# Moving steps within VectorE's and ScalarE's order at the batch ends of a Strassen pair loop

## The chip, the cores and the metric

One core of one Trainium2 chip. The metric is the device time of one execution in microseconds (us), lower is better. Engines are named as in the profile: PE (TensorE), DVE (VectorE), ACT (ScalarE), POOL (GpSimd), SP (SyncE, which issues the DMAs here).

## The reference

The input `x` is (8, 512, 64, 64) in float32. It is one attention block with pooled keys and values, all in float32:

```python
qk  = relu(bn(einsum('bchw,oc->bohw', x, qk_w)))      # 256 channels
val = relu(bn(einsum('bchw,oc->bohw', x, v_w)))       # 512 channels
key   = psp(qk)                       # adaptive max pools 1, 3, 6, 8: 110 cells
value = psp(val).transpose(0, 2, 1)
query = qk.reshape(B, 256, 4096).transpose(0, 2, 1)
scores = softmax(einsum('bnc,bcs->bns', query, key) * 256 ** -0.5)
y = einsum('bns,bsc->bnc', scores, value)             # to (B, 512, H, W)
return x + bn(einsum('bchw,oc->bohw', y, out_w))
```

## The kernel before

**Tiles.** Each of the 8 batches has 8 tiles of 512 positions, 64 tiles in all. Every float32 product is split into a high part (rounded to fp32r) and a low part (the rest), so one product of 128x128 weights with a 128x512 tile is three matmuls, hi*hi, lo*hi, hi*lo. ACT makes the high parts, POOL and DVE the low parts.

**Strassen pairs.** Tiles are taken two at a time, a pair step `s` from 1 to 27 (`PAIRS` is 28), and the convolutions of a pair are made with Strassen's scheme (Winograd's form) in three products `j` = 0, 1, 2 (two halves of the values' channels, then the queries' and keys'). `pair_product(s, j, fill1, ..., fill4)` is PE's order for one: P1 (3 matmuls), `fill1`, P5 (3), U2 (3), U1 (9), `fill2`, U3 (3), U5 (9), `fill3`, U6 (9), U7 (6), `fill4`. The fills are attention work of older tiles: `project` (probabilities times values times output weights, 3 matmuls), `sums` (row sums of the exponentials, 2), `scores` (6). Between them other engines make sums of PSUM banks: `copy_u1` and `copy_u5` (ACT, L851 and L857), `make_u4` (DVE, L1217), which U3 waits for, and `make_u7` (DVE, L1223), which U6 waits for before its first matmul.

**Attention** runs behind the convolutions: in step `s`, `A = 2s-8` and `B0 = A-1` are the tiles whose attention is done. For a tile `a`: `exps`, `split_e_lo` (L1286), `sums` (PE), `guess` (ACT, L925 and L927: a logarithm and an exponential give a reciprocal), `refine` (DVE, L1272 and L1275: one Newton step), `normalise` (L1281), `split_p_hi` (ACT, L931), `split_p_lo` (DVE, L1291), four `project`s, each followed by `add_out` (DVE, L1298), which adds the residual and frees the bank: `project(a, 2)` waits for `add_out(a, 0)`.

**Batch ends.** Where A is a multiple of 8 (s = 4, 8, 12, 16, 20, 24) a batch's tiles are complete (`batch_ended`). Then `finish_grids(VC, CC)` and `finish_keys` (L1237 to L1251) end the pooling of the keys, which `scores(A)` needs; `finish_grids(0, VC)` and `finish_values` end that of the values; PE multiplies values and output weights (`turn_values`, 12 matmuls, fill3 of j = 1), `make_values` (DVE), `values_hi` (ACT, L936) and `values_lo` (DVE, L1306) follow, and `project(A, 0)` (fill3 of j = 2) needs their result and `split_p_lo(A)`. Rows of each product are pooled by `pool_pair_rows` (DVE, L1157), groups of rows by `pool_cells` (L1195 to L1202). At s = 4 there is no `B0`.

**Loads of the pair.** `split_part_hi(s, i)` (ACT, L844) and `split_part_lo` (POOL, L449) split the nine parts of the next pair's data; POOL also makes four sums of tiles (L459 to L462, L468) and the queries' low part (L479). SP loads the next pair's tiles when part 6 and part 7 of this pair have their low part, and after that stores results and loads residuals in a ring of three buffers.

**Order.** Each engine's queue is in order, written out by hand as a list of calls per step; semaphores connect the engines. All of a step that an engine reaches waits behind what stands ahead of it in that list. Nothing plans the order at run time.

Of the kernel before, what the change touches and what calls it, by code (L numbers as in the profile page):

```python
# [26 lines left out]
def psp_attention(nc, x, qk_w, v_w, out_w, bn_in_rows, out):  # L27
# [14 lines left out]
    NT = 8  # L42
    TN = H * W // NT
    KC = CIN // P
    VC, QC, OC = CV // P, CK // P, CIN // P
# [13 lines left out]
    with ExitStack() as ctx:  # L59
# [748 lines left out]
        def _(act):  # L808
# [20 lines left out]
            def split_part_hi(s, i):  # L829

                raw, b0, b1 = PARTS[i]
                if i in (1, 2, 4, 8):
                    act.wait_ge(t_made, 4 * (s - 1) + {1: 1, 2: 2, 4: 3, 8: 4}[i])
                else:
                    wait_x(act, 2 * s + (1 if i in (5, 7) else 0))
                if s == 1:
                    if i not in (1, 2, 8):
                        act.wait_ge(conv_done, CC if i in (0, 3, 6) else 2 * CC)
                else:
                    n, g = product(s - 1, 2), pair_group(s - 1, 2)  # L840
                    used, count = [(p1_done, n), (p5_done, n), (u2_done, n), (conv_done, g), (u3_done, n),
                                   (conv_done, g + 1), (x0_used, n), (conv_done, g + 3), (conv_done, g + 2)][i]
                    act.wait_ge(used, count + 1)
                nc.scalar.activation(xh[:, b0:b1, :], raw, ACT.Copy).then_inc(x_hi, 1)  # L844

            def copy_u1(s, j):
                n = product(s, j)
                u1, _, u6, _ = pair_banks(n)
                act.wait_ge(p1_done, n + 1)
                act.wait_ge(rows_pooled, pair_group(s, j) - 2)  # L850
                nc.scalar.activation(u6[:, :], u1[:, :], ACT.Copy).then_inc(u1_copied, 1)  # L851

            def copy_u5(s, j):
                n = product(s, j)
                act.wait_ge(p5_done, n + 1)
                wait(act, u7_made, n)
                nc.scalar.activation(u5[:, :], pair_banks(n)[3][:, :], ACT.Copy).then_inc(u5_copied, 1)  # L857
# [63 lines left out]
            def guess(a):  # L921

                act.wait_ge(sums_done, a + 1)
                wait(act, p_made, a)
                nc.scalar.activation(r0[:, :], sum_ps[:, :], ACT.Ln).then_inc(ln_done, 1)  # L925
                act.wait_ge(ln_done, a + 1)
                nc.scalar.activation(r0[:, :], r0[:, :], ACT.Exp, scale=-1.0).then_inc(guess_made, 1)  # L927

            def split_p_hi(a):
                act.wait_ge(p_made, a + 1)  # L930
                nc.scalar.activation(e_slot(a)[0], score_bank(a)[:, :], ACT.Copy).then_inc(p_hi, 1)  # L931

            def values_hi(k):
                act.wait_ge(vo_made, k + 1)
                wait(act, out_done, OC * NT * k)
                nc.scalar.activation(vo_h[:, :], vo[:, :], ACT.Copy).then_inc(vo_hi, 1)  # L936
# [26 lines left out]
            for s in range(1, PAIRS):  # L963
                A = 2 * s - NT
                B0 = A - 1
                nxt = s + 1 if s + 1 < PAIRS else None
                copy_u1(s, 0)
                copy_u5(s, 0)
                if s > 1:
                    split_part_hi(s, 7)  # L970
                split_part_hi(s, 8)
                if B0 >= 0:
                    guess(B0)
                if A >= 0:
                    split_q_hi(A)
                if B0 >= 0:
                    split_p_hi(B0)
                copy_u1(s, 1)
                copy_u5(s, 1)
                if A >= 0:  # L980
                    exps(A)
                    split_q_hi(A + 1)
                if A >= 0 and A % NT != 0:
                    guess(A)
                    split_p_hi(A)
                copy_u1(s, 2)
                copy_u5(s, 2)
                if A >= 0 and A % NT == 0:
                    guess(A)
                    values_hi(A // NT)  # L990
                    split_p_hi(A)
                if nxt:
                    for i in range(4):
                        split_part_hi(nxt, i)
                store_pair_q(s, 0)
                if nxt:
                    split_part_hi(nxt, 4)
                    split_part_hi(nxt, 5)
                else:
                    split_hi(LAST, 0)  # L1000
                store_pair_q(s, 1)
                if A >= 0:
                    exps(A + 1)
                if nxt:
                    split_part_hi(nxt, 6)
                else:
                    split_hi(LAST, 1)
                store_pair_q(s, 2)
                store_pair_q(s, 3)
# [53 lines left out]
        def _(dve):  # L1063
# [277 lines left out]
            for s in range(1, PAIRS):  # L1341
                A = 2 * s - NT
                B0 = A - 1
                t0 = 2 * s % NT
                batch_ended = A >= 0 and A % NT == 0
                if s == 1:
                    pool_tile_cells(1, 0, CC)
                else:
                    pool_cells((t0 - 2) % NT, VC, CC, pair_group(s, 0))
                    pool_cells((t0 - 1) % NT, VC, CC, pair_group(s, 0))  # L1350
                make_u4(s, 0)
                if B0 >= 0:
                    refine(B0)
                    normalise(B0)
                pool_pair_rows(s, 0, 0)
                make_u7(s, 0)
                if A >= 2:
                    add_out(A - 2, 2)
                    add_out(A - 2, 3)
                if B0 >= 0:  # L1360
                    split_p_lo(B0)
                pool_pair_rows(s, 0, 1)
                if batch_ended:
                    finish_grids(VC, CC)
                    finish_keys()
                pool_pair_rows(s, 0, 2)
                pool_pair_rows(s, 0, 3)
                if B0 >= 0:
                    add_out(B0, 0)
                    add_out(B0, 1)  # L1370
                make_u4(s, 1)
                if batch_ended:
                    if B0 >= 0:
                        add_out(B0, 2)
                    finish_grids(0, VC)
                    finish_values(0, VC)
                    pool_pair_rows(s, 1, 0)
                    make_u7(s, 1)
                    split_e_lo(A)
                    pool_pair_rows(s, 1, 1)  # L1380
                    make_values(A // NT)
                    pool_pair_rows(s, 1, 2)
                    pool_pair_rows(s, 1, 3)
                else:
                    if A >= 0:
                        split_e_lo(A)
                    pool_pair_rows(s, 1, 0)
                    make_u7(s, 1)
                    if B0 >= 0:
                        add_out(B0, 2)  # L1390
                    pool_pair_rows(s, 1, 1)
                    if A >= 0:
                        refine(A)
                    pool_pair_rows(s, 1, 2)
                    if A >= 0:
                        normalise(A)
                    pool_pair_rows(s, 1, 3)
                    pool_cells(t0, 0, VC, pair_group(s, 2))
                    pool_cells(t0 + 1, 0, VC, pair_group(s, 2))
                    if A >= 0:  # L1400
                        split_p_lo(A)
                make_u4(s, 2)
                if B0 >= 0:
                    add_out(B0, 3)
                if batch_ended:
                    refine(A)
                    normalise(A)
                    pool_cells(t0, 0, VC, pair_group(s, 2))
                    pool_cells(t0 + 1, 0, VC, pair_group(s, 2))
                    values_lo(A // NT)  # L1410
                pool_pair_rows(s, 2, 0)
                make_u7(s, 2)
                if batch_ended:
                    split_p_lo(A)
                elif A >= 0:
                    add_out(A, 0)
                    add_out(A, 1)
                pool_pair_rows(s, 2, 1)
                if batch_ended:
                    add_out(A, 0)  # L1420
                if A >= 0:
                    split_e_lo(A + 1)
                pool_pair_rows(s, 2, 2)
                pool_pair_rows(s, 2, 3)
                if batch_ended:
                    add_out(A, 1)
# [119 lines left out]
```

## Time and profile before

| | us |
|---|---|
| median of 3 runs | 1461.75 (1459.16 to 1464.56) |
| the profiled execution | 1460.46 |
| its span, first to last instruction | 1458.7 |
| PE busy | 1371.6 (94%) |
| DVE busy | 973.6 (67%) |
| POOL busy | 753.5 (52%) |
| ACT busy | 632.2 (43%) |
| mean granted PE clock | 0.981 |
| DMA queues, share of 16 engines | 44% |

Matmuls are pipelined, each starts before the last has ended, so a busy PE is one that is being fed, and its rate is read from counts over a stretch.

### The profile page before, as it was taken

Reading aid. Unit: us, or ns where it says so; the run is one execution under the profiler, and the core shown is the slowest. Engines: PE = TensorE matmul, PEld = TensorE weight load, DVE = VectorE, ACT = ScalarE, POOL = GpSimd, SP = SyncE. Lnnn points to the kernel's source line nnn. Section 1 sums busy time; section 2 is a strip of 40 time slices with the busy share of each in tenths; the row PEclk is TensorE's granted clock in tenths of the full one; section 3 lists DMA queues with packets and bytes.
Section 4 is the critical chain, followed back from the end, with each engine's and each line's share of the span. In section 5 each row is a group of like instructions: output and inputs, shape, how many; then the busy total and the mean of one; then the engine's idle time right before and its main releaser. Section 6 shows DMA issues by size and latency. Waiting matters only on the chain. (4 is left out here: it accounts for less than half of the span.)

```text
span 1458.7 us, 17069 instructions
## 1 busy us (share of the span) xinstructions
PE 1371.6 (94%) x5786; PEld 1091.5 (75%) x5786; DVE 973.6 (67%) x2262; ACT 632.2 (43%) x991; POOL 753.5 (52%) x469
## 2 busy tenths in 40 slices
PE   7999889998899988999899997999979999999997
PEld 6777677786677867777677776777767777788885
DVE  6554567667667676676766766666766677877566
ACT  4233344542445524545245453345434454764422
POOL 2555566552655526555256552565524643675532
PEclk9999999999999999999999999999989999999999
DMA  5211144443444434544345442455424553898426
GB/s 188 87 58 58 58 145 144 142 144 101 162 156 141 137 109 151 166 141 133 110 144 173 151 144 81 144 173 165 143 69 144 173 173 116 275 317 274 145 87 231
DMA packets 110344, 213.46 MB, mean 146 GB/s; under 512 B 6538, under 2 KB 6578, under 8 KB 110258
## 3 DMA queue, kind: packets, MB, share of 16 engines
q1 hardware_dynamic: 109682, 211.33, 43.9%
q8 instruction: 46, 0.75, 0.2%
q10 hardware_dynamic: 576, 1.05, 0.2%
q14 instruction: 40, 0.33, 0.1%
HBM read 145.25 MB, written 67.11 MB: 146 GB/s over the span
## 5 line engine op out<-in xcount | busy, mean ns | idle before, releaser
L449 POOL TENSOR_TENSOR xl<-xa,xh 128x512 fp32r<-128x512 f32 x162 | 267.6, 1669 | 336.7 <-ACT xh L844 336.7
L1157 DVE TENSOR_REDUCE row_max<-conv_ps 128x64 f32<-128x384 f32 (+2 forms) x576 | 287.4, 529 | 212.2 <-ACT q L904 95.1
L570 PE MATMUL conv_ps<-xh,wh 128*128 128x512 f32 x891 | 353.9, 397 | 13.0 <-DVE conv_ps L1223 12.7
L572 PE MATMUL conv_ps<-xl,wh 128*128 128x512 f32 x891 | 350.1, 393 | 0.0
L571 PE MATMUL conv_ps<-xh,wl 128*128 128x512 f32 x891 | 348.7, 391 | 0.0
L479 POOL TENSOR_TENSOR q_l<-q,q_h 128x1024 fp32r<-128x1024 f32 x64 | 154.1, 2407 | 193.6 <-ACT q_h L910 193.6
L570 PEld LDWEIGHTS conv_ps<-xh,wh 128*128 128x128 f32 x891 | 168.9, 190 | 61.0 <-DVE conv_ps L1223 23.9
L572 PEld LDWEIGHTS conv_ps<-xl,wh 128*128 128x128 f32 x891 | 168.1, 189 | 37.5
L571 PEld LDWEIGHTS conv_ps<-xh,wl 128*128 128x128 f32 x891 | 168.7, 189 | 36.1
L851 ACT ACTIVATE conv_ps<-conv_ps 128x512 f32<-128x512 f32 x81 | 47.4, 585 | 260.2 <-PE conv_ps L572 260.2
L1298 DVE TENSOR_TENSOR xo<-out_ps,xo 128x512 f32<-128x512 f32 x226 | 148.2, 682 | 7.2 <-PE out_ps L663 6.4
L844 ACT ACTIVATE xh<-xa 128x512 fp32r<-128x512 f32 x162 | 123.9, 771 | 65.9 <-PE conv_ps L572 65.9
L570 PE MATMUL conv_ps<-xh,sh 128*128 128x512 f32 x324 | 133.3, 411 | 8.1 <-DVE row_max L1157 7.0
L661 PE MATMUL out_ps<-e_h,vo_h 128*128 128x512 f32 x218 | 91.3, 419 | 46.3 <-DVE e_l L1291 24.9
L572 PE MATMUL conv_ps<-xl,sh 128*128 128x512 f32 x324 | 129.2, 399 | 0.0
L571 PE MATMUL conv_ps<-xh,sl 128*128 128x512 f32 x324 | 128.9, 398 | 0.0
L1217 DVE TENSOR_TENSOR conv_ps<-conv_ps,u 128x512 f32<-128x512 f32 x81 | 56.4, 697 | 98.8 <-PE conv_ps L572 54.6
L443 POOL TENSOR_TENSOR xl<-xa,xh 128x1024 fp32r<-128x1024 f32 x34 | 81.5, 2409 | 62.1 <-ACT xh L827 62.1
L449 POOL TENSOR_TENSOR xl<-tt,xh 128x512 fp32r<-128x512 f32 x81 | 107.8, 1331 | 0.0
L857 ACT ACTIVATE u<-conv_ps 128x512 f32<-128x512 f32 x81 | 48.6, 599 | 113.0 <-PE conv_ps L572 112.9
L557 PE MATMUL conv_ps<-xh,wh 128*128 128x512 f32 x240 | 95.2, 397 | 0.0
L559 PE MATMUL conv_ps<-xl,wh 128*128 128x512 f32 x240 | 94.4, 393 | 0.0
(218 smaller groups left out, 2312.8 us busy)
## 6 DMA issues: line engine op xcount, KB each, us to landing
xa<-x SPq DMA_DIRECT2D x148, 512.0 KB, 4.6
xo<-x SPq DMA_DIRECT2D x115, 512.0 KB, 4.6
out<-xo SPq DMA_DIRECT2D x115, 512.0 KB, 3.1
q<-x SPq DMA_DIRECT2D x8, 512.0 KB, 4.6
out<-q SPq DMA_DIRECT2D x8, 512.0 KB, 3.2
q<-v_w ACTq DMA_DIRECT2D x4, 256.0 KB, 4.7
q<-out_w SPq DMA_DIRECT2D x1, 1024.0 KB, 6.9
out<-xa SPq DMA_DIRECT2D x2, 512.0 KB, 3.3
```

The costliest lines, as they stand in the source:

```text
L443: nc.gpsimd.tensor_tensor(xl[:, b:b + 2, :], xa[:, part, s % 2, :, :], xh[:, b:b + 2, :], ALU.subtract)\
L449: nc.gpsimd.tensor_tensor(xl[:, b0:b1, :], raw, xh[:, b0:b1, :], ALU.subtract).then_inc(x_lo, 1)
L479: nc.gpsimd.tensor_tensor(q_l[:, :, :], q[:, a % NT, :, :], q_h[:, :, :], ALU.subtract).then_inc(q_lo, 1)
L557: nc.tensor.matmul(bank(s, c)[:, :], wh[:, k, cols], hi, start=(k == 0), stop=False)
L559: last = nc.tensor.matmul(bank(s, c)[:, :], wh[:, k, cols], lo, start=False, stop=(k == KC - 1))
L570: nc.tensor.matmul(out[:, :], hi, xh[:, b, :], start=start, stop=False, skip_group_check=True)
L571: nc.tensor.matmul(out[:, :], lo, xh[:, b, :], start=False, stop=False, skip_group_check=True)
L572: return nc.tensor.matmul(out[:, :], hi, xl[:, b, :], start=False, stop=stop, skip_group_check=True)
L661: nc.tensor.matmul(bk[:, :], vo_h[:, cols], hi, start=True, stop=False)
L844: nc.scalar.activation(xh[:, b0:b1, :], raw, ACT.Copy).then_inc(x_hi, 1)
L1157: last = nc.vector.tensor_reduce(row_max[:, c, n, :], src[:, r0_ * W:r1_ * W].rearrange("p (r w) -> p w r", w=W), AX.X, ALU.max)
L1298: nc.vector.tensor_tensor(xt, out_bank(a, m)[:, :], xt, ALU.add).then_inc(out_added, 1)
```

## The change

Only the order of calls on two engines is changed, ACT (`block.scalar`) and DVE (`block.vector`); no instruction is added, removed or altered, and PE's, POOL's and SP's lists are the same.

On ACT: `copy_u5(s, 0)` goes behind part 7's split, `guess(B0)` ahead of part 8's; at batch ends `guess(A)` goes ahead of `copy_u1(s, 2)`, and parts 0 and 1 of the next pair go between `values_hi` and `split_p_hi(A)`. On DVE: at batch ends `finish_grids(VC, CC)` goes ahead of `refine(B0)`, `finish_keys` behind `add_out(B0, 0)` and `add_out(B0, 1)`, `refine(A)` ahead of `make_u4(s, 2)`, `values_lo` and `split_p_lo(A)` ahead of the cells' pooling. In every step `make_u7(s, 0)` goes directly behind `refine(B0)`.

```diff
--- before.py
+++ after.py
@@ -965,12 +965,12 @@
                 B0 = A - 1
                 nxt = s + 1 if s + 1 < PAIRS else None
                 copy_u1(s, 0)
-                copy_u5(s, 0)
                 if s > 1:
                     split_part_hi(s, 7)
-                split_part_hi(s, 8)
+                copy_u5(s, 0)
                 if B0 >= 0:
                     guess(B0)
+                split_part_hi(s, 8)
                 if A >= 0:
                     split_q_hi(A)
                 if B0 >= 0:
@@ -983,15 +983,21 @@
                 if A >= 0 and A % NT != 0:
                     guess(A)
                     split_p_hi(A)
+                batch_ended = A >= 0 and A % NT == 0
+                if batch_ended:
+                    guess(A)
                 copy_u1(s, 2)
                 copy_u5(s, 2)
-                if A >= 0 and A % NT == 0:
-                    guess(A)
+                if batch_ended:
                     values_hi(A // NT)
+                if nxt:
+                    split_part_hi(nxt, 0)
+                    split_part_hi(nxt, 1)
+                if batch_ended:
                     split_p_hi(A)
                 if nxt:
-                    for i in range(4):
-                        split_part_hi(nxt, i)
+                    split_part_hi(nxt, 2)
+                    split_part_hi(nxt, 3)
                 store_pair_q(s, 0)
                 if nxt:
                     split_part_hi(nxt, 4)
@@ -1349,25 +1355,27 @@
                     pool_cells((t0 - 2) % NT, VC, CC, pair_group(s, 0))
                     pool_cells((t0 - 1) % NT, VC, CC, pair_group(s, 0))
                 make_u4(s, 0)
+                if batch_ended:
+                    finish_grids(VC, CC)
                 if B0 >= 0:
                     refine(B0)
+                make_u7(s, 0)
+                if B0 >= 0:
                     normalise(B0)
                 pool_pair_rows(s, 0, 0)
-                make_u7(s, 0)
                 if A >= 2:
                     add_out(A - 2, 2)
                     add_out(A - 2, 3)
                 if B0 >= 0:
                     split_p_lo(B0)
                 pool_pair_rows(s, 0, 1)
-                if batch_ended:
-                    finish_grids(VC, CC)
-                    finish_keys()
                 pool_pair_rows(s, 0, 2)
                 pool_pair_rows(s, 0, 3)
                 if B0 >= 0:
                     add_out(B0, 0)
                     add_out(B0, 1)
+                if batch_ended:
+                    finish_keys()
                 make_u4(s, 1)
                 if batch_ended:
                     if B0 >= 0:
@@ -1399,25 +1407,29 @@
                     pool_cells(t0 + 1, 0, VC, pair_group(s, 2))
                     if A >= 0:
                         split_p_lo(A)
+                if batch_ended:
+                    refine(A)
                 make_u4(s, 2)
+                if batch_ended:
+                    normalise(A)
                 if B0 >= 0:
                     add_out(B0, 3)
                 if batch_ended:
-                    refine(A)
-                    normalise(A)
+                    values_lo(A // NT)
+                    split_p_lo(A)
+                    make_u7(s, 2)
+                    pool_pair_rows(s, 2, 0)
+                    pool_pair_rows(s, 2, 1)
                     pool_cells(t0, 0, VC, pair_group(s, 2))
                     pool_cells(t0 + 1, 0, VC, pair_group(s, 2))
-                    values_lo(A // NT)
-                pool_pair_rows(s, 2, 0)
-                make_u7(s, 2)
-                if batch_ended:
-                    split_p_lo(A)
-                elif A >= 0:
                     add_out(A, 0)
-                    add_out(A, 1)
-                pool_pair_rows(s, 2, 1)
-                if batch_ended:
-                    add_out(A, 0)
+                else:
+                    pool_pair_rows(s, 2, 0)
+                    make_u7(s, 2)
+                    if A >= 0:
+                        add_out(A, 0)
+                        add_out(A, 1)
+                    pool_pair_rows(s, 2, 1)
                 if A >= 0:
                     split_e_lo(A + 1)
                 pool_pair_rows(s, 2, 2)
```

## Rows read from the trace of the kernel before

**Rows 1.** The page, busy time of each engine.
```profile
PE 1371.6 (94%) x5786; PEld 1091.5 (75%) x5786; DVE 973.6 (67%) x2262; ACT 632.2 (43%) x991; POOL 753.5 (52%) x469
```

**Rows 2.** Waits of PE: us in total, times, longest us.
```profile
PE out_ps L661 <- DVE e_l L1291: 24.9, 7, 3.9
PE out_ps L661 <- DVE xo L1298: 21.4, 7, 4.2
PE conv_ps L570 <- DVE conv_ps L1223: 12.7, 23, 0.6
...
PE conv_ps L570 <- DVE row_max L1157: 7.0, 7, 2.6
```

**Rows 3.** Windows: stretch, its us, each engine's busy us (count), PEclk, DMA share, GB/s.
```profile
207.60:1192.40 984.80, 932.54 (x3910) 741.92 (x3910) 663.46 (x1520) 431.69 (x687) 518.84 (x331) 0.98 0.44 142
375.70:517.90 142.20, 140.01 (x601) 111.67 (x600) 97.83 (x225) 66.32 (x104) 81.57 (x52) 1.00 0.50 163
389.30:429.10 39.80, 39.80 (x173) 31.87 (x171) 26.64 (x62) 19.55 (x31) 21.94 (x16) 1.00 0.46 148
...
331.70:388.40 56.70, 47.96 (x187) 37.91 (x187) 37.20 (x89) 19.82 (x32) 23.97 (x16) 0.91 0.33 110
```

**Rows 4.** Timeline of PE at two batch ends (s = 24, s = 4): start, us, what.
```profile
1063.01 0.79 PE L661 MATMUL out_ps<-e_h,vo_h 128*128 128x512 f32 x1 [4.08 <-DVE xo L1298]
1063.60 0.63 PE L662 MATMUL out_ps<-e_h,vo_l 128*128 128x512 f32 x1
1064.03 0.63 PE L663 MATMUL out_ps<-e_l,vo_h 128*128 128x512 f32 x1
...
1080.46 0.39 PE L645 MATMUL sum_ps<-e_l,ones 128*128 128x512 f32 x1
...
1092.33 0.62 PE L661 MATMUL out_ps<-e_h,vo_h 128*128 128x512 f32 x1 [3.95 <-DVE e_l L1291]
...
190.23 0.50 PE L661 MATMUL out_ps<-e_h,vo_h 128*128 128x512 f32 x1 [3.54 <-DVE e_l L1291]
```

**Rows 5.** Timeline of ACT in step s = 24.
```profile
1044.62 0.58 ACT L851 ACTIVATE conv_ps<-conv_ps 128x512 f32<-128x512 f32 x1
1046.48 0.60 ACT L857 ACTIVATE u<-conv_ps 128x512 f32<-128x512 f32 x1 [1.28 <-PE conv_ps L572]
1046.98 1.05 ACT L844 ACTIVATE xh<-xa 128x1024 fp32r<-128x1024 f32 x1
...
1049.07 0.63 ACT L927 ACTIVATE r<-r 128x512 f32<-128x512 f32 x1
...
1082.97 0.60 ACT L857 ACTIVATE u<-conv_ps 128x512 f32<-128x512 f32 x1 [0.81 <-PE conv_ps L572]
```

**Rows 6.** Timeline of DVE in step s = 24.
```profile
1047.23 0.70 DVE L1217 TENSOR_TENSOR conv_ps<-conv_ps,u 128x512 f32<-128x512 f32 x1 [0.28 <-ACT u L857]
1049.73 0.70 DVE L1272 SCALAR_TENSOR_TENSOR sum_ps<-sum_ps,r 128x512 f32<-128x512 f32 x1 [1.80 <-ACT r L927]
...
1052.40 0.69 DVE L1223 TENSOR_TENSOR conv_ps<-conv_ps,u 128x512 f32<-128x512 f32 x1
...
1055.77 0.20 DVE L1238 TENSOR_TENSOR rows<-cells 128x36 f32<-128x36 f32 x1
1056.00 1.16 DVE L1239 TENSOR_TENSOR cells<-rows 128x18 f32<-128x18 f32 x1
1057.19 0.17 DVE L1240 TENSOR_REDUCE cells<-cells 128x2 f32<-128x18 f32 x1
...
1060.64 0.39 DVE L1251 TENSOR_TENSOR key_l<-key_d,key_h 128x220 fp32r<-128x220 f32 x1
...
1088.36 1.01 DVE L1202 TENSOR_REDUCE part<-row_max 128x8 f32<-128x88 f32 x6
```

**Rows 7.** Timeline of POOL in step s = 24.
```profile
1048.10 2.41 POOL L449 TENSOR_TENSOR xl<-xa,xh 128x1024 fp32r<-128x1024 f32 x1 [2.62 <-ACT xh L844]
...
1055.81 1.32 POOL L459 TENSOR_TENSOR tt<-xa 128x512 f32<-128x512 f32 x1 [1.69 <-DMA xa<-x]
```

## The prediction

> **What bounds the kernel.** First the page's busy times [rows 1]: PE is busy for 1371.6 of 1458.7 us, and the next engine, DVE, for 973.6. So the time is PE's work plus what PE waits, 87 us in all. Second, the waits of PE [rows 2]: two groups of seven, each with a longest wait near 4 us (behind `split_p_lo`, L1291, and behind `add_out`, L1298), 23 short ones of 0.6 us at most (U6 waiting for `make_u7`, L1223), and one of 2.6 us among those behind row pooling. Third, the windows [rows 3]. A stretch without a wait runs 173 matmuls in 39.80 us, 0.230 us each; a stretch with three of the short waits and one batch of ordinary steps takes 142.20 us with 140.01 busy for 601, 0.233 each. A step with a batch end takes 56.70 us for 187 matmuls, though 187 x 0.233 is only 43.6, and its granted clock is 0.91. Of the 13.1 us too many, 4.08 and 3.95 are the two long waits [rows 4] and 0.5 to 0.6 is the short one. The rest, some 4.5 us, is the clock: behind the wait the matmuls start 0.43 us apart (1063.60 to 1064.03), twice the usual distance, so TensorE has gone from 2.4 to 1.2 GHz after pausing some 4 us.
>
> **The first wait and its removal** (s = 24; the steps s = 8, 12, 16, 20 look alike). `project(B0, 2)` is ready 4.08 us before 1063.01, at 1058.93. Before it, DVE works off `finish_grids` and `finish_keys`, from before 1055.77 to 1061.03 [rows 6], then three row poolings and `add_out(B0, 0)`. After the change the grids fill a hole: behind `make_u4`, which starts at 1047.23, DVE now idles 1.80 us for `guess` [rows 6]. ACT's new order also makes `guess` sooner: it follows `copy_u5` at 1046.48 directly, so it ends at about 1046.48 + 0.5 + 1.2 = 1048.2 instead of 1049.7 [rows 5].
>
> What the grids cost there needs a look at POOL. L1239 took 1.16 us at 1056.00 and ended at 1057.16, 0.03 after POOL's L459 (1055.81 + 1.32 = 1057.13), while L1238 started before it and took 0.20 [rows 6, 7]. The reduction L1240 is not held. So such an instruction waits for the POOL instruction in flight. POOL's split of part 7 is issued 0.5 us behind `copy_u1` at 1044.62, and 1.05 us later POOL has it: 1046.2 to 1048.6 (2.41 us [rows 7]). L1237, at about 1047.83, then ends at 1048.7, L1238 runs to 1048.9, L1239 meets POOL's split of part 8 (from 1048.84, 1.3 us) and ends at 1050.2, L1240 at 1050.4. `refine` takes two steps of 0.73 us, `make_u7` 0.69: U7 is there at 1052.6. PE wants it at 1053.14 less 0.5, at 1052.65. The short wait shrinks to nothing, or to 0.1 to 0.2 us.
>
> Behind that, one instruction each 0.6 us: `normalise` 1052.5, a row, two `add_out`, `split_p_lo` until 1055.5, five row reductions until 1057.5, `add_out(B0, 0)` done at 1058.2. PE, 0.5 us earlier than before, wants it at 1058.4. The first long wait goes. `finish_keys` follows the second `add_out` at 1058.8. The next tiles' loads are issued when part 7 has its low part, now 1.9 us sooner, so POOL's L459 to L462 run from about 1054 to 1058 and no longer meet the keys, which take 3.6 us now (1057.36 to 1061.03 [rows 6]), two of them held as L1239 is; I estimate 1.7 us for six that aren't held, at 0.2 to 0.4 each as L1238 and L1251. They end at 1060.5, U2 at the same time, so `make_u4(s, 1)` isn't late, and `scores(A)` wants keys at 1062.4. Slack there is 1.9 us. `values` follow as before, with the `add_out(B0, 2)` ahead of them; its residual is loaded behind a store that DVE releases at 1054.9, and lands about 5 us later, against a use at 1061.2.
>
> **The second wait.** `project(A, 0)` waits for `split_p_lo(A)`. Its chain is `sums(A)`, `guess(A)` (1.2 us), `refine`, `normalise`, `split_p_hi`, `split_p_lo`. Today `guess(A)` stands behind `copy_u5(s, 2)` at 1082.97 [rows 5], which ends 2.7 us after `sums(A)` has; and between `split_p_hi` and `split_p_lo` DVE pools cells (the last six of them 1.01 us [rows 6], 2.3 in all), makes `values_lo`, waits for a row and makes U7. With the change `guess` starts when `sums(A)` is done, at about X = 1080.46 + 0.39 = 1080.85 [rows 4]. `copy_u1(s, 2)` is pushed back behind it, done at X + 1.8, where U2 wants it at X + 1.9. `refine` is done at X + 2.8 and `make_u4` starts at X + 2.9, as now. Then `normalise`, `add_out`, `values_lo` (perhaps held 0.5 us by POOL's split of part 0), `split_p_lo` done at X + 6.3, U7 at X + 6.9. PE ends U5 and wants the first at X + 7.5, the second 2 us later. The cells' 2.3 us lie behind the two row poolings then, with `split_e_lo(A+1)` behind them at about X + 13, and `sums(A+1)` wants it at X + 15. The second wait goes, and with it the slow clock.
>
> **Other steps.** 17 ordinary steps lie between 207.60 and 1192.40. There `guess` is 1.5 us sooner and `make_u7` right behind `refine`, so U7 is made when U3 is done, about 1.3 us before PE wants it. The 0.5 to 0.6 us wait goes in each.
>
> **The sum.** From 207.60 to 1192.40 PE runs 3910 matmuls [rows 3]. At 0.233 us each, a rate that still has short pauses in it, that is 911 us instead of 984.8: 74 us less. (At 0.230, without any, 900 and 85 less: the lower bound of the time.) The short wait of s = 5 just before gives 0.6. At s = 4 there is no `B0` and no fill of it: I count its second wait, 3.54 us [rows 4] and 1.4 of slow clock; its 2.6 us wait I count at nothing, since there POOL is late with four splits, the grids end near 159.5 and U6 waits about 2 us instead. Sum 74 + 0.6 + 5 = 79.6 us. The steps from s = 28 on and the start stay. 1460.5 - 79.6 = 1380.9. The profiled execution stands 1.3 us below the median of the runs, which is noise here: I say 1381.
>
> **A rule beside it.** POOL and DVE meet in the rows above. The Trainium skill, "SBUF — State Buffer", Who interferes with whom, says that a DVE instruction with two SBUF inputs, or in a two-port mode, and a GpSimd instruction lock each other out for the whole instruction, whoever comes first, and that reductions don't take part. It speaks against this change, which sets the grids into a stretch where POOL is at work; the trace agrees with it (L1239 held, L1240 not). Without such a lock the grids would end near 1048.7 and PE's waits would be as summed above.
>
> **Rivals.** *The grids are held twice.* L1238 starts about 0.1 us before POOL's split of part 8 in my working. If POOL is first, L1238 ends at 1050.2, and L1239 comes behind the start of POOL's 2.4 us for the queries and ends at 1052.6. Then U7 is at 1054.8, U6 waits 2.1 us, and all behind shifts with it. For: 0.1 us is thin. Against: the distances from `copy_u1` to `copy_u5` and `make_u4` that it hangs on come from engine chains and not from DMAs. Price 5 x 2.1 = 10.5 us: 1392. *One long wait comes back.* `copy_u1` behind `guess(A)` has 0.1 us of slack, `add_out(B0, 2)` and its residual under 1 us. If one of the two long waits stays in the five steps, with its clock, 5 x (4 + 2.2) = 31 us come back: 1412. *The waits only move.* If the chain behind them (keys, then values) was as late as they are, nothing is gained: 1461. Against it stands the slack of 1.9 us and more at each. *Slower: the clock.* With the pauses gone PE runs some 1000 us on end. If the chip took it to the lower level for part of that, each matmul would cost 0.43 - 0.23 = 0.2 us more; from 400 matmuls (of 3910) on the gain is eaten, at 450 the kernel is 10 us slower, 1471. Against: it held 1.00 through 601 matmuls from 375.70 to 517.90 [rows 3].
>
> **How the numbers follow.** Forecast 62%, grids held twice 22%, one wait back 11%, waits only move 3%, slower by the clock 2%. About 0.5% (7 us) is what a measurement can tell here. Both first cases and the third lie far below that line, so faster 0.95, same 0.03, slower 0.02. The range goes from 1371, a little above the bound with no pause at all (85 + 5.6 less is 1370), to 1402, past the 1392 of the first rival and halfway to the third case.
>
> **What would show it.** Right: PE's waits for L1298 and L1291 at batch ends gone from its list, those for L1223 under 3 us in total, PEclk 1.00 in batch steps of about 43.6 us, ordinary steps of 40.7, L1239 held once to about 1.2 us. Wrong: L1239 or L1238 at 2.4 us and U6 waiting 2 us behind L1223; or waits of PE at L570 (U2) for ACT L851, or new ones of 3 us and more anywhere with a clock of 0.9 behind them.

## The result and the profile after

| | before | after |
|---|---|---|
| median of 4 runs, us | 1462.55 | 1374.34 (1374.09 to 1377.43) |
| profiled execution, us | 1460.46 | 1374.09 |
| its span, us | 1458.7 | 1372.3 |
| mean granted PE clock | 0.981 | 0.999 |

The ratio is 0.9404, with a 95% interval from 0.9381 to 0.9427: 88.2 us less by the medians, 86.4 by the spans of the two profiled executions. 1381 was forecast, 1371 to 1402 was the range.

The page after, busy time of each engine (the answer to [rows 1]):

```profile
PE 1341.9 (98%) x5786; PEld 1077.6 (79%) x5786; DVE 967.1 (70%) x2262; ACT 633.3 (46%) x991; POOL 755.5 (55%) x469
```

The matmuls are the same. PE is busy for 30 us less (it ran some of them at the lower clock before) and idle for 57 us less. The waits of PE after, to be held against [rows 2] (L1163 is the old L1157, L1229 the old L1223, L1297 the old L1291, L1304 the old L1298):

```profile
PE conv_ps L570 <- DVE row_max L1163: 4.6, 7, 1.0
...
PE conv_ps L570 <- DVE conv_ps L1229: 2.2, 1, 2.2
...
PE out_ps L661 <- DVE e_l L1297: 1.7, 1, 1.7
...
PE out_ps L661 <- DVE xo L1304: 0.9, 2, 0.7
```

46.3 us of waiting for L1298 and L1291 have become 2.6, and the 23 short waits for U7 have become a single one. What is left for L1297 (1.7) stands in the first step behind the pairs, which the change does not touch. The windows after, for [rows 3] (stretch, its us, each engine's busy us and count, PEclk, DMA share, GB/s):

```profile
205.00:1109.90 904.90, 904.90 (x3909) 728.41 (x3908) 653.68 (x1518) 432.57 (x687) 520.88 (x330) 1.00 0.47 154
982.70:1026.20 43.50, 43.50 (x190) 35.09 (x189) 34.50 (x86) 20.06 (x33) 24.32 (x16) 1.00 0.39 129
1026.20:1066.70 40.50, 40.50 (x177) 32.63 (x176) 28.11 (x65) 19.59 (x32) 23.59 (x16) 1.00 0.53 177
```

In the first, all of 904.90 us is busy: through 3909 matmuls, five batch ends among them, the profile lists no wait of PE, and the clock is the upper one throughout. The second lies over a batch end, the third over an ordinary step. An ordinary step has 175 matmuls (the window counts two that its ends cut), so 40.50 us are 0.231 each; counted by their starts the batch end has the same 0.231.

How DVE goes through the batch end s = 24 after the change, and POOL beside it (start, us, what; for [rows 6, 7]):

```profile
978.11 0.70 DVE L1223 TENSOR_TENSOR conv_ps<-conv_ps,u 128x512 f32<-128x512 f32 x1 [0.28 <-ACT u L857]
978.71 0.91 DVE L1243 TENSOR_TENSOR cells<-part 128x72 f32<-128x72 f32 x1
979.66 0.20 DVE L1244 TENSOR_TENSOR rows<-cells 128x36 f32<-128x36 f32 x1
979.89 1.16 DVE L1245 TENSOR_TENSOR cells<-rows 128x18 f32<-128x18 f32 x1
981.08 0.17 DVE L1246 TENSOR_REDUCE cells<-cells 128x2 f32<-128x18 f32 x1
...
982.63 0.69 DVE L1229 TENSOR_TENSOR conv_ps<-conv_ps,u 128x512 f32<-128x512 f32 x1
```

```profile
977.12 2.42 POOL L449 TENSOR_TENSOR xl<-xa,xh 128x1024 fp32r<-128x1024 f32 x1 [0.75 <-ACT xh L844]
979.71 1.30 POOL L449 TENSOR_TENSOR xl<-tt,xh 128x512 fp32r<-128x512 f32 x1 [0.17 <-ACT xh L844]
```

L1243 meets POOL's split of part 7 and ends when that ends (979.54, 979.62). L1244 starts 0.05 us ahead of the split of part 8 and is free. L1245 meets that split and ends with it (1.16 us). The order of these three is the one worked out before, and its thin place is the 0.05 us. U7 is made at 983.32, and PE takes it up at once:

```profile
983.38 0.50 PE L570 MATMUL conv_ps<-xh,wh 128*128 128x512 f32 x1
983.72 0.40 PE L571 MATMUL conv_ps<-xh,wl 128*128 128x512 f32 x1
```

No wait is listed, but the second matmul stands 0.34 us behind the first and not 0.23, as it does behind a short wait. Since a matmul counts as busy for 0.39 us and the next one starts after 0.23, a pause of up to 0.16 us does not show as idle. So U7 comes just in time here, with nothing to spare.

### The profile page after: what moved, and what is told of

Same layout as the page of the kernel before. It is cut to its first block, busy times and chain, and to the rows that moved or that the text cites. A ratio compares the mean times of both kernels' runs of the same rounds, so it can differ in the third digit from the quotient of the medians.

```text
span 1372.3 us, 17075 instructions
## 1 busy us (share of the span) xinstructions
PE 1341.9 (98%) x5786; PEld 1077.6 (79%) x5786; DVE 967.1 (70%) x2262; ACT 633.3 (46%) x991; POOL 755.5 (55%) x469
## 4 chain that ended last, share of the span: by engine, by line
PE 88%; DVE 3%; ACT 1%; issue 1%; DVEq 0%; ACTq 0%
PE conv_ps L570 20%; PE conv_ps L572 19%; PE conv_ps L571 19%; PE out_ps L661 4%; PE out_ps L662 4%; PE out_ps L663 4%; PE conv_ps L559 3%; PE conv_ps L557 3%; PE conv_ps L558 3%; PE score_ps L634 2%; PE score_ps L633 2%; PE score_ps L632 2%; PE sum_ps L644 1%; PE sum_ps L645 1%; PE sum_ps L672 0%
## 5 line engine op out<-in xcount | busy, mean ns | idle before, releaser
L1163 DVE TENSOR_REDUCE row_max<-conv_ps 128x64 f32<-128x384 f32 (+2 forms) x576 | 285.5, 528 | 196.1 <-ACT q L904 91.2
L571 PE MATMUL conv_ps<-xh,wl 128*128 128x512 f32 x891 | 347.8, 390 | 0.0
L479 POOL TENSOR_TENSOR q_l<-q,q_h 128x1024 fp32r<-128x1024 f32 x64 | 154.1, 2408 | 175.6 <-ACT q_h L910 175.6
L1304 DVE TENSOR_TENSOR xo<-out_ps,xo 128x512 f32<-128x512 f32 x226 | 148.1, 681 | 1.6 <-PE out_ps L663 0.7
L925 ACT ACTIVATE r<-sum_ps 128x512 f32<-128x512 f32 x64 | 38.2, 596 | 146.8 <-PE sum_ps L645 146.8
L1223 DVE TENSOR_TENSOR conv_ps<-conv_ps,u 128x512 f32<-128x512 f32 x81 | 56.4, 696 | 66.8 <-PE conv_ps L572 55.9
L558 PE MATMUL conv_ps<-xh,wl 128*128 128x512 f32 x240 | 93.9, 391 | 0.0
```

The lines of the kernel that those rows point to most:

```text
L479: nc.gpsimd.tensor_tensor(q_l[:, :, :], q[:, a % NT, :, :], q_h[:, :, :], ALU.subtract).then_inc(q_lo, 1)
L558: nc.tensor.matmul(bank(s, c)[:, :], wl[:, k, cols], hi, start=False, stop=False)
L571: nc.tensor.matmul(out[:, :], lo, xh[:, b, :], start=False, stop=False, skip_group_check=True)
L1163: last = nc.vector.tensor_reduce(row_max[:, c, n, :], src[:, r0_ * W:r1_ * W].rearrange("p (r w) -> p w r", w=W), AX.X, ALU.max)
L1304: nc.vector.tensor_tensor(xt, out_bank(a, m)[:, :], xt, ALU.add).then_inc(out_added, 1)
```

## The experiments

Nine kernels start from the changed one, one from the kernel before, and two build on one of these. All medians are of four or five runs, and each ratio is to the kernel before, run beside it. Differences to the changed kernel (1374.34 us) are between medians taken at different times; the median of the kernel before moved by 1.3 us over them (1461.89 to 1463.21), so 1 to 2 us are not to be told apart.

### Undoing the order of keys and grids (first long wait)

```diff
                 make_u4(s, 0)
-                if batch_ended:
-                    finish_grids(VC, CC)
...
                 pool_pair_rows(s, 0, 1)
+                if batch_ended:
+                    finish_grids(VC, CC)
+                    finish_keys()
                 pool_pair_rows(s, 0, 2)
...
-                if batch_ended:
-                    finish_keys()
                 make_u4(s, 1)
```

> The changed kernel with finish_grids(VC, CC) and finish_keys back between the row poolings of product 0. Theory: the wait of project(B0, 2) for add_out comes back at 5 batch ends, 3.5 to 4 us each, 18 to 20 us, and with it the slow clock, up to 2.2 us each: 1393 to 1405. Rival, the first wait was removed by the sooner guess and make_u7 and not by the keys' place: under 3 us more.

Measured 1400.33 us (ratio 0.9575, 0.9561 to 0.9589): 26.0 more than the changed kernel. The wait is back in the list, 20.2 us, at most 4.3:

```profile
PE out_ps L661 <- DVE xo L1304: 20.2, 7, 4.3
```

### Undoing the order in product 2 (second long wait)

On ACT `guess(A)` goes back behind `copy_u5(s, 2)` and parts 0 and 1 behind `split_p_hi(A)`; on DVE the old block of product 2 stands again:

```diff
-                if batch_ended:
-                    refine(A)
                 make_u4(s, 2)
...
+                    refine(A)
+                    normalise(A)
+                    pool_cells(t0, 0, VC, pair_group(s, 2))
+                    pool_cells(t0 + 1, 0, VC, pair_group(s, 2))
+                    values_lo(A // NT)
+                pool_pair_rows(s, 2, 0)
+                make_u7(s, 2)
+                if batch_ended:
+                    split_p_lo(A)
```

> The changed kernel with the order of product 2 at batch ends as before, on both engines (guess(A) behind copy_u5, parts 0 to 3 behind split_p_hi(A), the cells ahead of values_lo). Theory: project(A, 0) waits again for split_p_lo(A), 4 us at 6 batch ends and 1.4 to 2.5 us of slow clock each: 1406 to 1413.

Measured 1409.18 us (0.9635, 0.962 to 0.9649), 34.8 more.

```profile
PE out_ps L661 <- DVE e_l L1291: 25.3, 7, 4.3
```

25.3 - 1.7 = 23.6 us of waiting are back at six batch ends, and 34.8 us of time. Most of the difference is the clock, see the doses below.

### What carries the short waits: three undoings and one edit alone

`make_u7(s, 0)` back behind `normalise` and the first row:

```diff
                     refine(B0)
-                make_u7(s, 0)
-                if B0 >= 0:
                     normalise(B0)
                 pool_pair_rows(s, 0, 0)
+                make_u7(s, 0)
```

> The changed kernel with make_u7(s, 0) back behind normalise and the first row. Theory: in ordinary steps the sooner guess alone keeps U7 on time (made 1.0 us before PE wants it), at 5 batch ends U7 is 1.2 us late behind grids and refine: 6 to 7 us more, 1381. Rival, make_u7's place carried the ordinary steps: 14 us more and above.

Measured 1381.12 us (0.9448, 0.9432 to 0.9464), 6.8 more; five waits of 1.16 to 1.18 us at batch ends and 2.79 at s = 4, none in an ordinary step.

ACT's first reorder undone:

```diff
-                if s > 1:
-                    split_part_hi(s, 7)
                 copy_u5(s, 0)
-                if B0 >= 0:
-                    guess(B0)
+                if s > 1:
+                    split_part_hi(s, 7)
                 split_part_hi(s, 8)
+                if B0 >= 0:
+                    guess(B0)
```

> The changed kernel with ScalarE's first reorder undone: copy_u5(s, 0) first, then parts 7 and 8, then guess(B0). Theory: in ordinary steps U7 is still made at about 1.9 us behind refine's start, 0.7 us before PE wants it, so nothing is lost there. At batch ends the grids meet GpSimd's split of part 7 instead of part 8: if L1238's successor gets in ahead of it, refine is 0.3 us late and nothing is lost, if not 1.6 us at 5 batch ends. 1374 to 1382. Rival, the sooner guess carried the gain of the short waits: 14 us more, 1388.

Measured 1375.71 us (0.9407, 0.9393 to 0.9421), against 1374.34: no difference that stands out. Five waits of 0.28 us came, and the one at s = 4 went.

Both undone:

> The changed kernel with both of these undone: ScalarE's first reorder (guess again behind parts 7 and 8) and make_u7(s, 0) directly behind refine. Theory, each alone keeps U7 on time in ordinary steps, so undoing both brings back what neither alone did: 0.8 us in 18 ordinary steps, and 1.5 to 2 us at 5 batch ends, 22 to 25 us: 1396 to 1400. Rival, the short waits went with the long ones: as the run with only make_u7 back, 1381 to 1383.

Measured 1402.54 us (0.9594, 0.9574 to 0.9614), 28.2 more, against 22 to 25 expected. The waits for U7:

```profile
PE conv_ps L570 <- DVE conv_ps L1229: 21.7, 23, 5.1
```

The 18 ordinary ones are 0.5 to 0.6 us long as in the kernel before, four batch ends have 1.60, and the fifth has 5.11. There DVE's three maxima lost their race against POOL (DVE, then POOL):

```profile
827.82 2.41 DVE L1243 TENSOR_TENSOR cells<-part 128x72 f32<-128x72 f32 x1
830.26 1.19 DVE L1244 TENSOR_TENSOR rows<-cells 128x36 f32<-128x36 f32 x1
831.49 2.26 DVE L1245 TENSOR_TENSOR cells<-rows 128x18 f32<-128x18 f32 x1
```

```profile
827.73 2.41 POOL L449 TENSOR_TENSOR xl<-xa,xh 128x1024 fp32r<-128x1024 f32 x1 [2.63 <-ACT xh L844]
830.10 1.30 POOL L449 TENSOR_TENSOR xl<-tt,xh 128x512 fp32r<-128x512 f32 x1
831.35 2.36 POOL L479 TENSOR_TENSOR q_l<-q,q_h 128x1024 fp32r<-128x1024 f32 x1
```

POOL's first instruction starts 0.09 us ahead of L1243, and each of the three waits for one whole POOL instruction: 5.9 us for what takes 0.6 unhindered. This is the rival "the grids are held twice" and one more, in one step of five. In the other four L1243 starts 0.26 to 0.28 us ahead of POOL and takes 0.22, L1244 0.20, and only L1245 is held (2.28 us).

The edit alone, on the kernel before:

```diff
                     refine(B0)
-                    normalise(B0)
-                pool_pair_rows(s, 0, 0)
                 make_u7(s, 0)
+                if B0 >= 0:
+                    normalise(B0)
+                pool_pair_rows(s, 0, 0)
```

> The kernel before with one edit: make_u7(s, 0) directly behind refine(B0). Theory: U6's short waits of 0.5 to 0.6 us and the restart behind them go in the 18 ordinary steps (41.3 us to 40.5 each), the long waits stay: 13 to 14 us less, near 1449. Rival, the short wait is caused by guess being late and not by make_u7's place: no change, 1462.

Measured 1443.25 us (0.9863, 0.9848 to 0.9878): 19.7 less than the kernel before beside it, 17.5 by the spans, more than the 13 to 14 expected. The short waits are gone. The first long wait grew from 21.4 to 24.8 us in sum, presumably since PE reaches it sooner and DVE does not:

```profile
PE out_ps L661 <- DVE xo L1298: 24.8, 7, 4.8
```

All of PE's waits in sum fell by 10.5 us (81.8 to 71.3). The rest goes with the number of waits, 23 fewer: each short wait costs some 0.27 us more than its listed length, 0.16 hidden in the busy time of the matmul before it and 0.11 at the restart. That is an estimate from the distances 0.23, 0.34 and 0.39 above, and it gives 10.5 + 23 x 0.27 = 16.7 of the 17.5.

So either of the two edits alone keeps U7 on time in ordinary steps, and only without both does it come late. Their effects do not add.

### Where the grids stand, and what holds them

`finish_grids(VC, CC)` directly ahead of `finish_keys`, behind the second `add_out`:

```diff
                 make_u4(s, 0)
-                if batch_ended:
-                    finish_grids(VC, CC)
...
                 if batch_ended:
+                    finish_grids(VC, CC)
                     finish_keys()
                 make_u4(s, 1)
```

> The changed kernel with finish_grids(VC, CC) directly ahead of finish_keys, behind both add_outs, so away from GpSimd's splits. Theory: keys are 0.8 us later, still before scores(A) want them, and U6's wait of 2.2 us at s = 4 goes: 1372. Rival, the place in ScalarE's hole was needed: scores(A) wait about 1 us at 5 batch ends, 1379.

Measured 1371.31 us (0.9379, 0.9364 to 0.9394), 3.0 less; the intervals of the two ratios overlap, but all four runs lie below all four of the changed kernel. The place in DVE's idle time behind `make_u4` was not needed: the keys have the slack. At s = 4 the wait moved, though: U6's 2.2 us went and `scores` wait 2.0 us for the keys.

```profile
PE score_ps L632 <- DVE key_l L1257: 2.6, 2, 2.0
```

Compared matmul by matmul, the profiled execution is 1.9 us ahead of the changed kernel's behind s = 4 and gains 0.4 us more at each of the five other batch ends, though neither profile lists a wait for U7 there: 0.1 us of it is the restart at U6 (the 0.34 us above), another 0.1 one of the same kind at 989.04, where `project` comes just behind `add_out`, and the rest is in smaller pieces. At s = 4 nothing is gained in waiting (2.0 for 2.2 us); what went are the slow matmuls that follow U6's wait in the changed kernel, see the clock below. The grids still meet POOL in three steps: L1243, L1244 and L1245 take 1.30, 1.29 and 1.20 us at s = 4, ahead of the keys that are late there, and L1243 0.51 and 0.78 at s = 16 and 20, where no wait comes of it.

The same maxima as reductions:

```diff
-grid_chain(nc.vector.tensor_tensor(g6, part6[:, cs, 0::2, :], part6[:, cs, 1::2, :], ALU.max))
+grid_chain(nc.vector.tensor_reduce(g6, part6[:, cs, :, :].rearrange("p c (r t) w -> p c r w t", t=2), AX.X, ALU.max))
```

and in the same way for `rows3` and `g3`.

> The changed kernel with the grids' three maxima of two tensors written as reductions of one tensor over pairs, which have one SBUF input. Theory: they aren't held by GpSimd's instruction in flight, take about 0.2 to 0.3 us each also at L1245 and at s = 4, and U6's wait of 2.2 us at s = 4 goes: 1372. Rival, they are held as well (then the hold isn't one of the second input): 1374 or above.

Measured 1370.24 us (0.937, 0.9356 to 0.9384), 4.1 less, the best median here. At s = 8 (DVE, then POOL):

```profile
316.28 0.30 DVE L1243 TENSOR_REDUCE cells<-part 128x72 f32<-128x144 f32 x1
316.61 0.23 DVE L1244 TENSOR_REDUCE rows<-cells 128x36 f32<-128x72 f32 x1
316.87 0.19 DVE L1245 TENSOR_REDUCE cells<-rows 128x18 f32<-128x36 f32 x1
```

```profile
314.71 2.40 POOL L449 TENSOR_TENSOR xl<-xa,xh 128x1024 fp32r<-128x1024 f32 x1 [0.76 <-ACT xh L844]
```

POOL is at work from 314.71 to 317.11, over all three, and they take 0.30, 0.23 and 0.19 us. With two SBUF inputs the same work took 0.91, 0.20 and 1.16 in this step of the changed kernel.

This edit changes two things at once, the number of SBUF inputs and the kind of instruction. The traces tell them apart. In the changed kernel all 226 additions of `add_out` (L1304, `xo<-out_ps,xo`, a TENSOR_TENSOR with one input in PSUM and one in SBUF) take 0.68 to 0.69 us, though 159 of them start while a POOL instruction is under way. So a TENSOR_TENSOR is held by its second SBUF input. But one SBUF input is not free in every form: the keys' TENSOR_SCALAR instructions take 0.27 to 0.28 us alone and are held as well, here in the kernel with the reductions at s = 4 (DVE, then POOL):

```profile
162.62 1.33 DVE L1252 TENSOR_SCALAR key_d<-key 128x110 f32<-128x110 f32 x1
```

```profile
162.59 1.28 POOL L461 TENSOR_TENSOR tt<-xa,tt 128x512 f32<-128x512 f32 x1
```

It is the reduction that no POOL instruction held in any of these profiles.

### How a wait is priced: doses

Row reductions of a constant tile, 0.6 us each, are set ahead of `split_p_lo(A)` at the six batch ends of the changed kernel, five or nine of them. They add work that computes nothing of the result.

```diff
+                    hold(9)
                     split_p_lo(A)
```

where `hold(n)` holds

```diff
+                for i in range(n):
+                    nc.vector.tensor_reduce(pad[:, i:i + 1], shift_bc[:, :], AX.X, ALU.max).then_inc(held, 1)
```

> The changed kernel with nine row reductions of a constant tile (0.6 us each) on VectorE ahead of split_p_lo(A) at the 6 batch ends: 5.4 us of delay, of which about 1.1 is slack, a wait of 4.3 us for project(A, 0), 26 us in all. If a pause of that length brings the clock to its lower level behind it, as in the kernel before, 6 times 2.2 more: 1413 to 1415. If the long waits' price is their length alone: 1400.

> The changed kernel with five row reductions of a constant tile (0.6 us each) on VectorE ahead of split_p_lo(A) at the 6 batch ends, where nine gave waits of 4.1 us and cost 35 us. 3.0 us of delay, of which 1.1 is slack, give a wait of about 1.8 us for project(A, 0), 11 us in all. Theory, a pause that short leaves the clock at its upper level: 1385 to 1387. Rival, every wait costs clock in proportion (35 us for 24.5 us of waiting): 1390.

Nine: 1409.54 us (0.9642, 0.9622 to 0.9661); five: 1387.91 us (0.9493, 0.9475 to 0.9511). By the spans (1407.3, 1386.2, 1372.3) that is 35.0 and 13.9 us for 24.2 and 9.9 us of waiting (25.9 and 11.6, less the 1.7 of the changed kernel). PE behind the wait with nine, then with five:

```profile
362.29 0.80 PE L663 MATMUL out_ps<-e_h,vo_h 128*128 128x512 f32 x1 [4.12 <-DVE e_l L1308]
362.88 0.63 PE L664 MATMUL out_ps<-e_h,vo_l 128*128 128x512 f32 x1
363.31 0.63 PE L665 MATMUL out_ps<-e_l,vo_h 128*128 128x512 f32 x1
```

```profile
356.20 0.50 PE L663 MATMUL out_ps<-e_h,vo_h 128*128 128x512 f32 x1 [1.73 <-DVE e_l L1308]
356.53 0.40 PE L664 MATMUL out_ps<-e_h,vo_l 128*128 128x512 f32 x1
356.77 0.40 PE L665 MATMUL out_ps<-e_l,vo_h 128*128 128x512 f32 x1
```

Behind 4.12 us the distance is 0.43 us (362.88 to 363.31, the 1.2 GHz level), behind 1.73 us it is 0.24. The long wait costs 35.0 / 6 = 5.8 us, 4.0 of them the wait itself. The 1.8 above it can be read from the starts: the first two matmuls are 0.59 us apart (0.36 too many), six more 0.43 (1.2 in all), one 0.33 (0.1), and 0.16 are hidden in the busy time before the wait. The short one costs 0.27 us above its 1.65, the same 0.16 and a restart of 0.34 for 0.23 us; none of the six has a slow matmul in the 6 us behind it. That makes 9.9 + 1.6 = 11.5 of the 13.9 us. Of the other 2.4, 2.2 are eleven slow matmuls elsewhere in that profile, seven of them near its end behind a wait of 1.9 us that the changed kernel has too, there without any: chance, and not the dose's.

### Two attempts beyond

On top of the reductions, the last pair's values' grids finished sooner:

```diff
                         add_out(A, 1)
+                    if s == PAIRS - 1:
+                        finish_grids(0, VC)
                     pool_pair_rows(s, 2, 1)
...
                     finish_keys()
-                    finish_grids(0, VC)
                     finish_values(0, VC)
```

> The changed kernel with the grids as reductions (one SBUF input), and the values' grids of the last pair's batch finished in the idle time before that pair's last row poolings and not behind the keys of the step after. The wait of the values' product there (1.48 us) shrinks by 1.2 us: 1369, against 1370 for the reductions alone. Rival, the rows behind the grids become late: 1370 or more.

Measured 1373.83 us (0.9396, 0.9378 to 0.9414): 3.6 more than with the reductions alone. The wait for the values fell to 0.2 us, but the next one, for `split_p_lo`, grew from 1.7 to 4.0 us, with seven slow matmuls behind it. The cause is in DVE's and POOL's timeline there:

```profile
1157.81 2.61 DVE L1312 TENSOR_TENSOR vo_l<-vo,vo_h 128x512 fp32r<-128x512 f32 x1
```

```profile
1157.53 2.34 POOL L479 TENSOR_TENSOR q_l<-q,q_h 128x1024 fp32r<-128x1024 f32 x1 [4.59 <-ACT q_h L910]
```

With the reductions alone `values_lo` (L1312, two SBUF inputs) started at 1158.01, POOL's L479 at 1158.12, and it took 0.68 us. Now L1312 starts 0.20 us sooner and L479 0.59, so POOL is first by 0.28 us, and DVE stands for 2.6. So the last attempt puts `values_lo` of that step ahead of `refine`:

```diff
+                if s == LAST + 1:
+                    values_lo(ap // NT)
                 refine(ap)
                 normalise(ap)
...
-                if s == LAST + 1:
-                    values_lo(ap // NT)
                 split_e_lo(ac)
```

> The run with the last grid sooner, plus values_lo of the step after the pairs moved ahead of refine. In that run values_lo (two SBUF inputs) started 0.28 us behind GpSimd's low part of the queries, took 2.61 us and not 0.68, and the wait of project for split_p_lo there grew from 1.66 to 3.96 us. Theory, the lock: ahead of refine it meets no GpSimd instruction, takes 0.7 us, the wait falls to 1.2 to 1.6 us and the 1.3 us gained at the values' product show in the end: 1.8 us below the run with the reductions alone, 1368.4. Rival, the wait grew for another reason: 1370 or more.

Measured 1371.10 us (0.9363, 0.9341 to 0.9385; 1368.72 to 1372.53), granted clock between 0.995 and 1.000. L1312 takes 0.68 us there again:

```profile
1155.17 0.68 DVE L1312 TENSOR_TENSOR vo_l<-vo,vo_h 128x512 fp32r<-128x512 f32 x1
```

The lock is gone as supposed, but the wait for `split_p_lo` is 2.2 us and not 1.2 to 1.6, again with seven slow matmuls behind it, and the version is not shown to beat the reductions alone (1370.24). Its fastest two runs, at clock 1.000, are 1368.7 and 1368.9, its others stand at 0.995 to 0.997.

## Why the prediction was right

**The sum.** Both profiles have the same 5786 matmuls in the same order, so the saved time can be read at each of them:

| stretch (of the kernel before) | counted, us | measured, us |
|---|---|---|
| up to the first P5 of s = 4 (151.65) | 0 | 1.2 |
| from there to the first U6 of s = 5 (207.69) | 5.6 | 4.3 |
| the 3910 matmuls to 1192.5 | 74 | 79.3 |
| behind them | 0 | 1.7 |
| sum | 79.6 | 86.5 |

Each of the two long waits goes by the edit meant for it: undone, the one brings back 26.0 us and the other 34.8. Undoing `guess` and U7 together gives 28.2, and the three add up to 89.0 of the 88.2 us. That they meet so well is luck: the 28.2 contain one wait of 5.1 us with slow matmuls and four of 1.6, which the kernel before does not have, and the same short waits were worth 19.7 us where they were taken out alone.

**The rate was the mis-sized term.** "At 0.233 us each, a rate that still has short pauses in it, that is 911 us": measured were 905.6 us for the 3910, 0.2316 each. These 5.4 us are most of the 6.7 between 1381 and 1374.3. The stretch that the rate came from had short waits in it (four, where the prediction says three), and its busy time left out their listed length but not the 0.27 us beside each: without these 4 x 0.27 = 1.1 us, 140.01 would give 0.231. The other rate, 0.230 from 39.80 us, was too low because the window's count of 173 includes matmuls cut by its ends; only 171 start in it. That the truth lay in the middle between the two is luck.

**The ends** were counted at nothing and gave 1.2 and 1.7 us. In the 1.7 are five slow matmuls (1.0 us) near 1435 in the kernel before, behind a wait of 1.9 us that both kernels have and behind which the changed one has none; that is chance, as far as these profiles tell.

**The first wait** went. For s = 24, U7 was worked out for 5.37 us behind the start of `make_u4(s, 0)` (1052.6 less 1047.23) and came at 5.21 (983.32 less 978.11); which of the three maxima are free and which are held came out as worked out. The reading that "the reduction L1240 is not held" was no test, though: it started at 1057.19, 0.01 us ahead of POOL's next instruction. The run with reductions is the test. That the grids had to stand there was not claimed, and the run with them late shows that they need not.

**The second wait** went: `split_p_lo(A)` was expected 6.3 us behind the end of `sums(A)`, with 1.2 us of slack.

```profile
1004.25 0.60 ACT L925 ACTIVATE r<-sum_ps 128x512 f32<-128x512 f32 x1 [7.26 <-PE sum_ps L645]
```

```profile
1009.82 0.68 DVE L1297 TENSOR_TENSOR e_l<-score_ps,e_h 128x512 fp32r<-128x512 f32 x1
```

```profile
1011.62 0.39 PE L661 MATMUL out_ps<-e_h,vo_h 128*128 128x512 f32 x1
```

It ended 1010.50 less 1004.25 = 6.25 us behind, and 1.1 us ahead of `project(A, 0)`.

**At s = 4** the 2.6 us wait was to be replaced by one of about 2 us for U7. It was 2.18, behind three holds of 1.74, 1.18 and 2.27 us. From its first P5 to the first U6 of s = 5, 56.0 us (151.65 to 207.69) became 51.7 (150.46 to 202.19), 4.3 less for 5.6 counted. The 1.3 us missing are about one slow clock: the sum has 1.4 us of it going with the second wait and none for the wait that takes its place. But behind that one seven matmuls run at the lower level, from 1.1 us after the restart:

```profile
159.04 0.50 PE L570 MATMUL conv_ps<-xh,wh 128*128 128x512 f32 x1 [2.18 <-DVE conv_ps L1229]
159.38 0.40 PE L571 MATMUL conv_ps<-xh,wl 128*128 128x512 f32 x1
...
160.14 0.63 PE L571 MATMUL conv_ps<-xh,wl 128*128 128x512 f32 x1
160.56 0.63 PE L572 MATMUL conv_ps<-xl,wh 128*128 128x512 f32 x1
```

**The clock.** Forecast was that the slow matmuls go with the long waits: the clock is 1.00 throughout the stretch. The doses say the same from the other side. The slower rival, a clock that falls because PE never pauses, is refuted by 904.90 us without a listed wait at 1.00. Overlooked was that the wait of some 2 us left at s = 4 can bring it down too.

**The rule that spoke against the change** was not decisive: the holds cost 1.7 us of DVE's time per batch end, most of it while DVE would have been idle, up to some 0.4 us of PE's there, and at s = 4 2.2 us of PE's and the slow matmuls behind them. L1245 ends with POOL's instruction, and the reductions pass it by. The Trainium skill ("SBUF — State Buffer", Who interferes with whom) has both, the hold for two SBUF inputs and none for reductions, and these runs agree with it. The rival built on it, the grids held twice and more, did not happen at the five batch ends of the changed kernel. It happened at its s = 4, where about that was expected, and in one step of five when both short-wait edits were undone; in the first attempt beyond, the same lock met `values_lo`.

**One claim of the text was too simple.** It gave the end of the ordinary short waits to the sooner `guess` and to `make_u7`'s place together. Each does it alone; the runs with one undone cost 1.4 us (not distinguishable) and 6.8 (the batch ends), with both 28.2.

## What to carry to other kernels

When the busiest engine waits for a result, list what stands ahead of that result in its maker's queue, and move what has slack behind it: here no instruction was saved, and 6% of the time went. Price a wait of that kind not by its length alone, but look at the starts of the matmuls behind it. Take the rate for the forecast from starts over a long stretch, and not from a window's busy time and count: the first hides short pauses, the second counts matmuls that the ends cut. Where a DVE instruction with two SBUF inputs meets POOL, its duration depends on who started first, and 0.1 us can decide over 2; writing a small maximum as a reduction took the race away here. One SBUF input alone is not the rule, since the keys' TENSOR_SCALAR instructions were held with one.

## What the runs showed that was not expected

The three short DVE instructions took 0.6 us unhindered and up to 5.9 us in a row when each met a whole POOL instruction. With the same kernel and place it was so in one step of five only: POOL started 0.09 us before them there, and 0.26 to 0.28 us behind them in the other four.

And the length of a wait does not alone decide whether the clock falls behind it. In the 14 profiles together, from 20 us on, the slow matmuls (0.43 us apart) in the 6 us behind a wait of PE:

| wait, us | where | slow matmuls behind it |
|---|---|---|
| 1.2 to 1.7 | 40 waits, among them the six doses of five reductions | none |
| 1.9 | near the end of all 14 profiles | none in six, 5 to 8 in eight |
| 2.0 | grids late, s = 4 | none |
| 2.2 | s = 4 in four profiles, `split_p_lo` in the last attempt | 7 or 8 in all five, from 1.1 to 1.6 us after the restart |
| 2.6 | the kernel before, s = 4 | none |
| 2.8 | U7 back alone, s = 4 | 5, from 0.6 us after the restart |
| 3.5 to 5.1 | 41 waits, at batch ends and in the first attempt beyond | 5 to 13 |

Waits of 1.2 to 1.7 us left the clock alone, and from 2.8 us on every wait brought it down. Between them it went either way, and what decides there stays open.
